# Cross attention: softmax weights transposed as 64-row tiles around each unit of scores, four PSUM banks in one rotation, an order for each group of heads

## The reference, cut to what matters

```python
x = _layernorm(x + self_attention(x))           # 16 heads of 64, norms on q and k, tanh clamp
def cross(x, context):                          # the block that the change is in
    q, k, v = heads(x @ Wq), heads(context @ Wk), heads(context @ Wv)    # 16 heads of 64
    sim = einsum('bhid,bhjd->bhij', q, k) * 64 ** -0.5                   # 224 x 750 for each head
    out = einsum('bhij,bhjd->bhid', softmax(sim), v)
    return merge(out) @ Wo + bo
x = _layernorm(x + cross(x, ctx_768))
x = _layernorm(x + feed_forward(x))             # ternary weights, inner width 2048
```

## Time and profile before

| what | value |
|---|---|
| median of three runs | 1943.18 us (1940.18 to 1943.33) |
| the profiled execution | 1947.31 us |
| its span, first to last instruction | 1945.7 us |
| mean granted TensorE clock | 0.982 of full speed |
| front and group 0 of cross attention | about 640 us to 1160 us of the span |
| group 1 and its last batch | about 1160 us to 1757 us |

### The profile page before, as it was taken

One profiled execution on the slowest core, in us unless ns is written; L12 is line 12 of the kernel. 1 busy time (PEld: TensorE's weight loads), 2 busy tenths in 40 slices (PEclk: granted clock), 3 DMA queues, 4 the chain that ended last, 5 costly groups with the idle time before them and its releaser, 6 DMA issues.

```text
span 1945.7 us, 39197 instructions
## 1 busy us (share of the span) xinstructions
PE 1847.2 (95%) x12618; PEld 1514.6 (78%) x12618; DVE 1471.7 (76%) x3326; ACT 1172.2 (60%) x2568; POOL 999.7 (51%) x1065
## 2 busy tenths in 40 slices
PE   5999998999998999999999999999999999988997
PEld 4777776777776898899899888888888888874443
DVE  5677677788888777777777777877777777777887
ACT  5676776675675466566656666655555555554664
POOL 0343443244343266665675644567677667540554
PEclk9899999999997999999999999999999999999999
DMA  4321323011113414322431432313332331252221
GB/s 127 125 71 61 103 80 105 29 38 47 29 46 108 153 46 139 120 93 96 140 99 62 158 104 60 104 49 92 107 87 64 84 107 44 66 125 72 65 65 60
DMA packets 109571, 166.76 MB, mean 86 GB/s; under 512 B 32488, under 2 KB 67672, under 8 KB 109512
## 3 DMA queue, kind: packets, MB, share of 16 engines
q1 hardware_dynamic: 91016, 129.77, 21.7%
q0 software_dynamic: 14656, 28.92, 5.2%
q10 hardware_dynamic: 3840, 7.34, 1.3%
...
## 4 chain that ended last, share of the span: by engine, by line
PE 56%; DVE 16%; issue 11%; ACT 5%; POOL 5%; DMA 5%; POOLq 0%; SPq 0%; DVEq 0%; ACTq 0%
PE att_ps_P L1477 9%; PE att_ps_P L1489 9%; PE att_ps_T L1523 7%; PE att_ps_O L1537 6%; PE att_ps_SA L1512 5%; PE att_ps_O L1548 4%; PE att_ps_P L1466 4%; PE att_ps_T L451 3%; DVE sa_sums L751 2%; PE att_ps_SB L513 2%; DMA out_dram<-ff_y_out 2%; DVE ca_big L1772 2%; DVE att_ps_O L1904 1%; DMA sa_ff_in<-in_L_ffn_w_gate_dram 1%; PE att_ps_P L468 1%
## 5 line engine op out<-in xcount | busy, mean ns | idle before, releaser
L1345 POOL TENSOR_TENSOR ca_pr<-ca_pr,ca_rec 112x750 f32<-112x750 f32 x256 | 364.2, 1440 | 249.6 <-DVE ca_rec L1767 247.0
L392 POOL TENSOR_TENSOR sa_p_lo<-sa_pr,sa_p_hi 112x448 fp32r<-112x448 f32 x128 | 147.9, 1161 | 330.2 <-ACT sa_p_hi L599 330.2
L1657 ACT ACTIVATE ca_big<-att_ps_T 126x448 fp32r<-126x448 f32 x374 | 204.0, 546 | 137.9 <-PE att_ps_T L1523 134.0
L1772 DVE TENSOR_TENSOR ca_big<-att_ps_T,ca_big 126x448 fp32r<-126x448 f32 x374 | 231.8, 620 | 36.3 <-ACT ca_big L1657 28.4
L1489 PE MATMUL att_ps_P<-ca_w_hi,ca_ct 128*126 128x256 f32 x1152 | 236.8, 290 | 4.7 <-DVE ca_v_st L1755 4.2
L1523 PE MATMUL att_ps_T<-att_ident,ca_pr 112*126 112x112 f32 x1496 | 211.9, 263 | 8.0 <-DVE ca_big L1772 6.2
L1477 PE MATMUL att_ps_P<-ca_ct,ca_w_hi 128*128 128x376 f32 x768 | 201.4, 343 | 0.0
L1523 PEld LDWEIGHTS att_ps_T<-att_ident,ca_pr 112*126 112x126 f32 x1496 | 159.6, 140 | 51.7 <-issue 26.6
L1489 PEld LDWEIGHTS att_ps_P<-ca_w_hi,ca_ct 128*126 128x126 f32 x1152 | 185.5, 187 | 15.8 <-issue 8.5
L1537 PE MATMUL att_ps_O<-ca_big,ca_v_st 126*128 126x448 f32 x756 | 183.6, 378 | 5.8 <-DVE ca_big L1772 3.0
L1489 PE MATMUL att_ps_P<-ca_w_lo,ca_ct 128*126 128x256 f32 x576 | 162.3, 282 | 0.0
...
## 6 DMA issues: line engine op xcount, KB each, us to landing
...
```

What stands on the lines that cost most here:

```text
L392: pool.tensor_tensor(p_lo[:, h % NB, :], pr[:, h % NB, :], f32(p_hi[:, h % NB, :]), ALU.subtract).then_inc(p_split, 1)
L1345: pool.tensor_tensor(w, w, rec[:, h % PB, c:c + 1].to_broadcast([R, S]), ALU.mult).then_inc(norm_done, 1)
L1657: act.activation(weights_view(h, t, False), blocks_view(source.bank, t), ACT.Copy).then_inc(t_hi_done, 1)
L1772: dve.tensor_tensor(weights_view(h, t, True), blocks_view(source.bank, t), f32(weights_view(h, t, False)), ALU.subtract).then_inc(source.d ...
```

## The change

T units become T*h*.*c*, one for each half `c` of the query rows, so 16 for a batch and group where there were 24. Each is 12 transposes in 6 pairs: rows 0 to 63 of the six blocks into one bank (tile `a`, 6 x 64 = 384 columns), rows 64 to 111 into another (tile `b`, 6 x 48 = 288 columns). ACT and DVE drain `a` and `b` apart, four drains for each head where there were three. All orders put a T unit directly ahead of and directly behind each unit of scores (`T4.0 S3.0 T5.0`). P0, P1, T and O become one rotation of four banks (`TURN`) for all units but the scores, in the order in which the PE makes them; `~` skips a bank. There is one order for each group and engine (`ORDERS`), picked by the group of the batch ahead. On POOL the sum of the first pair of heads (B0) moves from the head of the step to before N4.0 of the next batch, and the reload of x (KX) moves ahead of N0.1. The last batch uses the same rotation, with O5 and O7 in SB and Y1 in SA. The splits of the next group's weights are tied to other units, and the ternary loads of the last batch wait for V15 of the batch before. The front takes T0.0 after Q2, and its wait for the end of self attention's norm moves from O0 to T0.0.

```diff
-                "T0.0": [drained_last("P2"), (ff_meaned, 1)], "O0": [(y_done, 2 * B)]}.get(u, [])
+                "T0.0": [drained_last("P2"), (ff_meaned, 1), (y_done, 2 * B)]}.get(u, [])
...
+    ROWS = {"a": slice(0, HALF), "b": slice(HALF, R)}
+    TURN = ("P0", "P1", "T", "O")
...
+    ORDERS = [steps("""XT0+ XT1+ T2.1 S2.1 T3.1 Q0+ Q1+ CT00+ O2 CT01+ CT02+ O3 CT10+ CT11+ V00+ CT12+ Q2+ T4.0 S3.0 T5.0 V01+
+                      K00+ V02+ T4.1 S3.1 T5.1 K01+ O4 V03+  ~  O5 T6.0 S0.0+ T7.0 K10+ V04+ Q3+ T6.1 S0.1+ T7.1 K11+ K20+ O6
+                      V05+ O7 T0.0+ S1.0+ T1.0+ V10+ K21+ Y0 V11+ T0.1+ S1.1+ T1.1+ Y1 O0+ V12+ O1+ T2.0+ S2.0+ T3.0+ K30+
+                      K31+ V13+ V14+ V15+  ~"""),
+              steps("""T2.1 S2.1 T3.1 Q0+ Q1+ O2 O3 T4.0 S3.0 T5.0 K00+ Q2+ V00+ T4.1 S3.1 T5.1 K01+ O4 K10+ O5  ~  V01+ V02+
+                      T6.0 S0.0+ T7.0 Q3+ K11+ V03+ K20+ T6.1 S0.1+ T7.1 K21+ V04+ O6 O7 V05+ V10+ T0.0+ S1.0+ T1.0+ Y0 T0.1+
+                      S1.1+ T1.1+ Y1 O0+ V11+ O1+ T2.0+ S2.0+ T3.0+ K30+ V12+ V13+ V14+  ~  K31+ V15+""")]
+    LAST = steps("""T2.1 S2.1 T3.1 O2 O3 T4.0 S3.0 T5.0 T4.1 S3.1 T5.1 O4 T6.0 O5 T7.0 x! T6.1 O6 ~ T7.1 u0! O7 u1! ~ ~ Y0 Y1
+                    u2! u3!""")
...
-        def transpose_weights(h, t, at, place):
-            to = place(f"T{h}.{t}", at)
+        def transpose_weights(h, c, at, st):
+            tiles = [(st(f"T{h}.{c}{x}"), rows) for x, rows in ROWS.items()]
+            for to, _ in tiles:
+                pe.wait_ge(to.free, to.nth_free)
+            pe.wait_ge(norm_done, at(2 * HG, nth(h, c)))
+            pe.sem_inc(t_begun, 1)
+            for j in range(JC):
+                for to, rows in tiles:
+                    width = rows.stop - rows.start
+                    mm = pe.transpose(to.bank[0:J, j * width:j * width + width], pr[rows, h % PB, c, J0[j]:J0[j] + J], ident[rows, rows])
+                    if j == JC - 1:
+                        mm.then_inc(to.filled, 1)
-            pe.wait_ge(to.free, to.nth_free)
-            if t < 2:
-                pe.wait_ge(norm_done, at(2 * HG, nth(h, t)))
-            for n, (j, c) in enumerate(BLOCKS[t]):
-                mm = pe.transpose(to.bank[0:J, n * R:n * R + R], pr[:, h % PB, c, J0[j]:J0[j] + J], ident[0:R, 0:R])
-            mm.then_inc(to.filled, 1)
...
-        def weights_hi(h, t, at, place):
-            source = place(f"T{h}.{t}", at)
+        def weights_hi(h, c, x, at, st):
+            source = st(f"T{h}.{c}{x}")
             act.wait_ge(source.filled, source.nth_filled)
-            act.activation(weights_view(h, t, False), blocks_view(source.bank, t), ACT.Copy).then_inc(t_hi_done, 1)
+            act.activation(weights_view(h, c, x, False), blocks_view(source.bank, x), ACT.Copy).then_inc(t_hi_done, 1)
```

DVE's order around a pair of T units in group 1 after the change, and POOL's for both groups:

```diff
+  ... T4.0a T4.0b M6.0 M7.0 T5.0a T5.0b R6.0 R7.0 K00+ Q2+ V00+ T4.1a T4.1b M6.1 M7.1 T5.1a T5.1b R6.1 R7.1 K01+ O4 K10+ O5 ...
-  B0 N4.1 N5.1 FR0 B1 FC0 N6.0 N7.0 FT0 N6.1 N7.1 FR1 B2 FC1 N0.0+ N1.0+ FT1 N0.1+ N1.1+ FR2 B3 FC2 KX N2.0+ N3.0+ FT2 N2.1+ N3.1+ N4.0+ N5.0+ KC
+  N4.1 N5.1 FR0 B1 FC0 N6.0 N7.0 FT0 N6.1 N7.1 FR1 B2 FC1 N0.0+ N1.0+ FT1 KX N0.1+ N1.1+ FR2 B3 FC2 N2.0+ N3.0+ FT2 N2.1+ N3.1+ B0+ N4.0+ N5.0+ KC
```

More of the change, by code:

```diff
@@ L1021, in cross_attention @@
-    CACHED = ("XT", "CT")
-    plans, front = [banks(UNITS), banks([u for u in UNITS if u[0:2] not in CACHED])], banks(FRONT)
-    last_units = UNITS[UNITS.index("V10"):]
-    assert sorted(FRONT) == sorted(UNITS) and FRONT[-len(last_units):] == last_units
+    CACHED = ("XT", "CT")
+    ROWS = {"a": slice(0, HALF), "b": slice(HALF, R)}
+    TURN = ("P0", "P1", "T", "O")
+    FRONT = steps("""S1 CT00+ XT0+ O0 O1 S2 O2 S3 O3 O4 O5 O6 XT1+ O7 total CT01+ CT02+ CT10+ Y0 CT11+ CT12+ Y1 Q0+ K00+ K01+
+                     K10+ S0.0+ K11+ Q1+ K20+ S0.1+ K21+ Q2+ T0.0+ S1.0+ T1.0+ Q3+ V00+ V01+ V02+ V03+ T0.1+ S1.1+ T1.1+ V04+
+                     V05+ ~+ K30+ O0+ V10+ O1+ K31+ V11+ T2.0+ S2.0+ T3.0+ V12+ V13+ V14+ V15+""")
@@ new lines, in kind_of @@
+    def kind_of(order, kinds):
+        return [name for name, _ in order if name[0] in kinds]
+    UNITS = [kind_of(order, "XCQKV") for order in ORDERS]
+    FRONT_UNITS = kind_of(CROSS_FRONT, "XCQKV")
+    assert sorted(FRONT_UNITS) == sorted(UNITS[0]) and sorted(UNITS[1]) == sorted(u for u in UNITS[0] if u[0:2] not in CACHED)
+    front_plan, plans, last_plan = banks(CROSS_FRONT, TURN[0:2], "T0.0"), [banks(order) for order in ORDERS], banks(LAST, own={"O5": "SB", "O7": "SB", "Y1": "SA"})
+    LOOPS = [B - 1, B]
@@ new lines, in uses, with uses_before, uses_in_all, __init__ @@
+    def uses(plan, s):
+        return plan.uses.get(s, 0)
+    def uses_before(plan, s):
+        n = B * GROUPS * HG if s in ("SA", "SB") else 0
+        for earlier, times in ((front_plan, 1), (plans[0], LOOPS[0]), (plans[1], LOOPS[1])):
+            if earlier is plan:
+                break
+            n += times * uses(earlier, s)
+        return n
+    def uses_in_all(s):
+        return uses_before(last_plan, s) + uses(last_plan, s)
+    class Step:
+        def __init__(self, plan, count):
+            self.plan, self.count = plan, count
+        def __call__(self, u):
+            s = self.plan.slot[u]
+            n = self.count(uses(self.plan, s), uses_before(self.plan, s) + self.plan.nth[u])
+            return Place(psum[s], filled[s], n + 1, drained[s], n + 2, drained[s], n + 1)
@@ L1026, in batch, with step_of, order_of @@
+    at_front_step, at_last_step = Step(front_plan, lambda per, k: k), Step(last_plan, lambda per, k: k)
+    def step_of(b, g):
+        if g == 0 and isinstance(b, int) and b == B - 1:
+            return Step(plans[1], lambda per, k: k)
+        return Step(plans[g], lambda per, k: b * per + (g * per + k))
+    def order_of(orders, ahead):
+        return orders[ahead.group]
     def batch(b, g, ahead=0):
@@ L1285, in rest @@
             load_weights(0, WP, W)
[L1286 to L1287 removed]
+            keep_x(0, at_front_step)
+            keep_context(0, at_front_step)
             for g in range(GROUPS):
@@ L1526, in values @@
-        def values(h, at, place):
-            to, source = place(f"O{h}", at), [place(f"T{h}.{t}", at) for t in range(3)]
-            pe.wait_ge(to.free, to.nth_free)
-            for n, s in enumerate(source):
-                if all(s.drained is not later.drained for later in source[n + 1:]):
-                    pe.wait_ge(s.drained, s.nth_drained)
-            if h % VH == 0:
-                v = f"V{h // VH}{JC - 1}"
-                pe.wait_ge(drained[slot_of(v, at)], drained_count(v, at))
+                            mm.then_inc(filled[scores_slot(h)], 1)
@@ L1585, in first, with front @@
                 pe.wait_ge(w_done, weights_for(0)[name])
-            do(name, at_front)
+            do(name, at_front, at_front_step)
+        def front(last):
+            for name, of_cross in FRONT:
+                if of_cross:
+                    first(name)
+                elif name != "~":
+                    last(name)
         def rest(ff_first):
@@ L1599, in rest @@
                 else:
-                    do(name, batch(B - 1, GROUPS - 1), at_end)
-        return first, rest
+                    do(name, batch(B - 1, GROUPS - 1), at_last_step)
+        return front, rest
     def scalar(act):
@@ L2422, in _ @@
             last = sa.tensor(pe)
-            first, rest = ca.tensor(pe)
+            front, rest = ca.tensor(pe)
             ff_first, ff_rest = ff.tensor(pe)
-            turn("""S1 CT00+ XT0+ O0 O1 S2 O2 S3 O3 O4 O5 O6 XT1+ O7 total CT01+ CT02+ CT10+ Y0 CT11+ CT12+ Y1 Q0+ K00+ K01+ K10+ S0.0+
-                    K11+ Q1+ S0.1+ T0.0+ K20+ K21+ S1.0+ T0.1+ Q2+ Q3+ T0.2+ V00+ V01+ S1.1+ T1.0+ V02+ V03+ T1.1+ V04+ V05+ T1.2+ S2.0+
-                    V10+ K30+ O0+ T2.0+ K31+ V11+ T2.1+ V12+ V13+ T2.2+ V14+ V15+ O1+""", last, first)
+            front(last)
             rest(ff_first)
```

465 lines of the change are left out of this document (215 added, 250 removed).

## The result

The changed kernel takes **1922.9 us** (median of 4 runs, 1918.7 to 1926.5) where the kernel before took 1943.3 in runs on the same chip (1940.2 to 1943.4): a ratio of 0.9898, 95% interval 0.9876 to 0.992. In a second set it stood at 0.9883 (0.9865 to 0.99). The forecast was 1882 us with a range of 1858 to 1916, so the sign was right and the range missed.

A forecast was written before the change was run, and what follows sets the result against it. The PE's string of units was taken to bound the kernel: -52.5 (units) - 14 (old waits) + 5 (new waits) = -61.5 us, from a median of 1943.2 to 1882 us, range 1858 to 1916.

The forecast's parts named there:

- The unit term: On the PE, a T S T group falls from 2.56 to 2.15 us; 128 groups save 52.5 us.
- Rival C: 64-row transposes on the PE pace at 0.106 us a pair, a group takes 2.65 us: 1946, no change; chance 0.02.
- Rival E: Changes of tiles on the PE cost more, scores to transposes being a full change: 1905 us; chance 0.05.
- I add 5 us for new waits: PE waiting for late banks behind DVE's drains: 5 us added, bounds 0 and 20.
- Of the 20.3 us I take 14 as gone: PE waits for the T units' one bank and a V bank: 14 of 20.3 us vanish, bounds 5 and 20.
- half a microsecond: Bank margin: DVE finishes in 4.3 us with nothing late; the third unit behind the group wants the bank at 4.8.
- Rival A: Part of the gain turns into waits on DVE's strict queue, 81% busy: 1895 to 1927 us; chance 0.15.
- Its stores wait for the same drains, which move with the PE: SP's queue: stores follow drains that move with the PE; no cost in the sum.
- The tail keeps what its PE units save and no more: Last batch: ternary loads hang on V15 and the previous batch's store, so only PE unit savings remain.
- Rival B: Kept context reaches K00 late in group 1, at worst 2.7 us in 7 batches: 1901 us; chance 0.05.
- Rival D: Slower: a group's second T waits for DVE, 1.87 us in three of eight groups: 1972 us; chance 0.05.
- the three signs of error that were named: Wrong if a batch exceeds 68 us, a pair paces at 0.1 us, or PE waits for DVE pass 40 us.

The follow-up runs named there:

- the early load alone: Changed kernel with group 1's load of a batch's first feed-forward block issued ahead of the store of the rows before it: 1923.0 us, ratio 0.9889.
- experiment 1: Changed kernel, DVE's group 1 order: two layernorm links moved ahead of a reciprocal, the last ones behind the drains of V13, V14 and K31: 1941.8 us, ratio 0.9979.
- experiment 2: Changed kernel with only the last layernorm link (F14) in DVE's group 1 order moved from behind V12's drain to behind K31's: 1957.8 us, ratio 1.0061.
- experiment 3: Changed kernel, DVE's group 1 order: four layernorm links ahead of the first reciprocal, the last link (F14) behind V14's drain: 1931.3 us, ratio 0.9925.
- the best kernel: Changed kernel with experiment 3's order, bias additions between V12's and O1's drains, feed-forward maximum behind O7's drain, and the block's load ahead of the store: 1894.6 us.
- experiment 4 with the order of experiment 3: Changed kernel with experiment 3's DVE order and group 1's first feed-forward block load ahead of the store: 1906.4 us, ratio 0.9787.

## Why the forecast was right in its sign and wrong in its size

**The unit term held.** Said: 0.41 us a group, eight groups a batch, so 3.3 us. Group 0: 69.4 - 3.3 + 0.95 (T2.0 for O0) + 0.4 (T2.1 for V15's bank, the fifth row of waits) = 67.5; measured 67.4. Group 1 with the links out of the way and the loop cut: 64.1, where "about 64" was said. The pace (0.06), the joint (0.36 us to the scores), the drains (0.55 and 0.45 us on DVE, 0.49 and 0.41 on ACT, from 256 tiles of each width) all came as worked out. Rivals C and E are out.

**The step that failed** is the term "I add 5 us for new waits". Its neighbour, "Of the 20.3 us I take 14 as gone", was too small: neither of its two rows is left in the view of PEld's waits from 640 to 1745 us. Nor did these waits lie in group 1 and the front alone: 5.8 us of them stood in the switch batch. The new waits came to far more than 5: eight waits of K31 and the half clock behind them about 26 us (3.2 each, as the batch of 67.3 and that of 64.1 say), T2.0 and T2.1 in group 0 about 10, T3.0 in group 1 about 4 (fourth row), and the last batch 7.2 over its old length instead of some 3 under it. The eighth wait of K31 lies in the last batch, so some 3 of these 50 us are counted twice. With 47 for the 5, and all 20 of the old waits gone, the sum gives about -25; the two profiled executions differ by 24.0 and the medians by 20.4. The margin of "half a microsecond" was computed for an undisturbed DVE, for a bank three units on. What it left out is what else stands in DVE's queue ahead of that drain, and that these items do not last what their mean says: a link behind a reciprocal lasts as long as GpSimd's product. The means of the kernel before held the hint, since the two-operand link of line 1904 took 0.41 us where its neighbours took 0.15, and no step read it.

**Rival A was the outcome.** Part of the gain turned into waits on DVE's strict queue, at 1895 to 1927, and it came at that range's top. It got 0.15, and the range gave up precisely its upper third. Its "For" was the right argument. Its price counted the wait alone, without the clock, which adds 1.4 us to K31's 2.0 where it falls.

**"Its stores wait for the same drains, which move with the PE"** was right for the changed kernel (the early load alone gives nothing) and wrong as a reason to stop looking: the store's release had about a microsecond to spare in group 1, and experiments 1 to 3 lost 9 to 35 us by it.

**"The tail keeps what its PE units save and no more"** was wrong by about 10 us. It looked at the loads that hang on V15 and not at DVE's item ahead of T6.1's drains, which waits for a load with a time of its own: when the PE gets faster and the DMA does not, the item turns into a wait.

**Rival B** (kept context late) did not come: no wait of that kind is in the view of the PE's waits. It did in experiments 1 and 2, where K00 waited about 1 us for that load in each steady batch (5.8 and 5.9 us in all). **Rival D** had the place nearly right, waits before T2.0 and T3.0, at 1 us in one group of eight instead of 1.87 in three. Of the three signs of error that were named, one came in full: the PE's waits for DVE stand at 44.5 us. The batches stayed under 68 us but for one of 68.1.

**What was left in the best kernel.** The first batch of group 1 still took 67.9 us. K31 waits there too (2.2 us), and no experiment moved what it waits for. Ahead of V12's drain DVE has splits of the next group's weights, which take 0.69 us by themselves and here ran beside GpSimd's products:

```profile
1218.52 1.38 DVE L1738 SCALAR_TENSOR_TENSOR ca_w_lo<-ca_stage,ca_w_hi 128x512 fp32r<-128x512 f32 x1 [0.35 <-ACT ca_w_hi L1628]
...
1220.28 1.46 DVE L1738 SCALAR_TENSOR_TENSOR ca_w_lo<-ca_stage,ca_w_hi 128x512 fp32r<-128x512 f32 x1
```

So "the same 14 chunks at other units: nothing" was wrong for these two. With the same wait this batch took 66.6 us in the run of experiment 4 with the order of experiment 3, at a clock of 1.00, and 67.9 here at 0.97. What decides whether the clock falls stays open. So does the front, where new waits for drains took what the units saved (732.8 us to the first Y0, before 732.2): no experiment touched it.
